# A new cycle for each pair of image rows: denominator first, double PSUM buffers, the Newton step in place

## The chip, the cores and the metric

The kernel runs on one core of a Trainium2 chip. Its engines are TensorE (PE, matmuls into the accumulator memory PSUM), VectorE (DVE), ScalarE (ACT), GpSimd (POOL), and the queue that issues transfers (SP). Each runs its own instruction stream in order, and they meet at semaphores. The metric is device time in microseconds (us); less is better.

## The reference

Two equal layers work on x of shape (2, 256, 256, 384): batch, rows h, width w, channels c, in float32. Each normalizes in 32 groups of 12 channels and adds a ratio of box sums:

```
def _gn(v, G=32, eps=1e-5):               # mean and variance over (h, w, channels of a group)
    return ((g - m) / jnp.sqrt(s + eps)).reshape(v.shape)
def conv(x):                              # windows (1, 5, 20) over h, w, c
    s = box_sum(x, 2, 5)
    num = box_sum(s * s, 3, 20)
    d = box_sum(box_sum(x * x, 2, 5), 3, 20)
    return nan_to_num(num / (d * norm))   # norm: how many columns the window of 5 covers
x = x + conv(_gn(x));  x = x + conv(_gn(x))
```

## The kernel before, in words

There are four phases: two layers times two images. A phase walks through 128 pairs of rows; four pairs make a tile, which is loaded and stored in one transfer of 3 MB. One pair is 128 partitions by 4 segments (two rows, each in two halves of the width) by 384 channels.

For one pair, POOL subtracts the group means (`centred`, L323). ACT squares it (`square`, L382). PE sums along the width: three S units on the centred rows and three T units on the squares, one per 128 channels, each into a width bank of PSUM (`width_unit`, L482). ACT copies these out, S squared and scaled into `sT` (L401), T scaled into `tT` (L398). PE sums along the channels (`channel_unit`, L506): four D units from `tT` into the denominator banks, four N units from `sT` into the numerator banks, one per segment. ACT forms a first reciprocal of the denominator by Ln and Exp (`invert`, L411 and L414). DVE makes one Newton step and the product: `approach` (L668) writes denominator times reciprocal into `newton`, `weigh` (L674) multiplies the numerator into `recip`, and `divide` (L686) writes (newton - 2) * recip, the negative ratio, for the whole pair into `y_out`. POOL subtracts it from the input (`add_ratio`, L332), and SP stores the tile.

The order of each engine is written out by hand as a list of names in its `step`: S, T, D, N as above with the number of the unit, F for parts of the next phase's statistics, L for invert, Q for squares. Channel units of a pair are mixed with the width units of the next pair. A float32 matmul of the program stands in the trace as two.

Apart from that DVE gathers group statistics with BATCH_NORM_STATS instructions, for the phase after next. In the first layer it measures each output tile (`measure_output`), eight groups per pair. In phase 0 it also measures the second image's input (`measure_beside`), eleven, eleven and ten groups in three pairs of four. At a few places `lane_totals` (BATCH_NORM_AGGREGATE) sums up what was gathered. Once per phase `ask_means` and `finish` turn this into the next phase's means and scales, with small matmuls (F1, F2, F3) and two activations (`finish_logs`). In the first 306 us only the first image is measured.

## Time and profile before

| | us |
|---|---|
| median of 3 runs | 6079.46 (6078.21 to 6080.62) |
| the profiled execution | 6080.48 |
| its span in the trace | 6078.8 |

The span runs from the first instruction to the last. A time in the trace counts from its start, and "L506" is line 506 of the kernel before. Matmuls overlap each other, so that the sum of their mean durations is above PE's busy time; weight loads (PEld) run beside them. The clock column is the part of 2.4 GHz that TensorE was granted.

### The profile page before, as it was taken

How to read it: one execution, taken by the hardware profiler on the slowest of the kernel's cores; microseconds unless marked ns; L12 is line 12 of the kernel's file. 1: busy time of each engine (PE TensorE's matmuls, PEld its weight loads, DVE VectorE, ACT ScalarE, POOL GpSimd, SP SyncE). 2: the span in 40 equal slices, each digit the busy share in tenths (PEclk: the TensorE clock that was granted, in tenths of full speed). 3: DMA queues.
4: the chain of work that ended last, by engine and by line, in shares of the span. 5: the costliest groups of instructions: out<-in, count | busy, mean ns of one | idle time of the engine just before them, and what ended most of it. 6: DMA issues, size and time to landing. Idle time of an engine off the chain costs nothing.

```text
span 6078.8 us, 138073 instructions
## 1 busy us (share of the span) xinstructions
PE 5725.4 (94%) x49196; PEld 5713.1 (94%) x49196; DVE 4097.6 (67%) x8521; ACT 5015.7 (83%) x8201; POOL 3547.4 (58%) x1043
## 2 busy tenths in 40 slices
PE   0099999999999999999999999999999999999999
PEld 0099999999999999999999999999999999999999
DVE  7888889988877676766767555555555555555555
ACT  0088888888888888888888888888888888888888
POOL 0056665566656666666665666666666666666665
PEclk9999999999999999999999999999999999999999
DMA  9956565556533434434344343343434434343343
GB/s 358 346 205 215 203 214 200 205 202 215 207 125 125 163 127 143 146 124 162 128 143 147 125 153 137 135 155 124 164 126 145 146 126 164 124 155 135 135 154 124
DMA packets 664736, 1007.80 MB, mean 166 GB/s; under 512 B 5168, under 2 KB 664624, under 8 KB 664624
## 3 DMA queue, kind: packets, MB, share of 16 engines
q1 hardware_dynamic: 664624, 1006.65, 47.2%
q14 instruction: 84, 0.69, 0.0%
q8 instruction: 28, 0.46, 0.0%
HBM read 603.98 MB, written 402.65 MB: 166 GB/s over the span
## 4 chain that ended last, share of the span: by engine, by line
PE 89%; DVE 6%; DMA 2%; issue 1%; ACT 1%; SPq 0%; POOL 0%; DVEq 0%; POOLq 0%; ACTq 0%
PE width_ps L482 43%; PE den_ps L506 23%; PE num_ps L506 23%; DVE out_stats L571 2%; DMA y_both<-in_x_dram 1%; DVE lane_mv L578 1%; DMA x_both<-in_x_dram 1%; DVE y_both L686 1%; DVE newton L668 1%; DVE recip L674 0%; DVE beside_stats L571 0%; DVE lane_mv L584 0%; SPq L204 0%; ACT recip L411 0%; ACT recip L414 0%
## 5 line engine op out<-in xcount | busy, mean ns | idle before, releaser
L323 POOL TENSOR_TENSOR centred<-x_both,mean_row 128x1536 f32<-128x1536 f32 x512 | 1771.5, 3460 | 1405.8 <-PE width_ps L482 1091.4
L332 POOL TENSOR_TENSOR y_both<-x_both,y_both 128x1536 f32<-128x1536 f32 x512 | 1771.7, 3460 | 1119.0 <-DVE y_both L686 1119.0
L668 DVE SCALAR_TENSOR_TENSOR newton<-den_ps,recip 128x384 f32<-128x384 f32 x2048 | 1112.5, 554 | 1883.5 <-ACT recip L414 1853.8
L506 PE MATMUL den_ps<-band_c,tT 128*128 128x138 f32 (+2 forms) x12288 | 1809.4, 283 | 10.7 <-DVE newton L668 10.3
L506 PE MATMUL num_ps<-band_c,sT 128*128 128x138 f32 (+2 forms) x12288 | 1732.9, 284 | 21.0 <-DVE recip L674 20.9
L482 PE MATMUL width_ps<-band_w,centred 128*128 128x130 f32 x12288 | 1629.7, 275 | 2.9 <-POOL centred L323 2.9
L482 PE MATMUL width_ps<-band_wc,square 128*128 128x130 f32 x12288 | 1625.7, 275 | 0.7 <-ACT sT L401 0.7
L506 PEld LDWEIGHTS den_ps<-band_c,tT 128*128 128x128 f32 x12288 | 1609.5, 190 | 14.5 <-DVE newton L668 12.3
L506 PEld LDWEIGHTS num_ps<-band_c,sT 128*128 128x128 f32 x12288 | 1580.8, 190 | 28.0 <-DVE recip L674 23.4
L401 ACT ACTIVATE sT<-width_ps,rstd_col 128x512 f32<-128x512 f32 x1536 | 1036.7, 675 | 591.6 <-PE width_ps L482 589.9
L482 PEld LDWEIGHTS width_ps<-band_w,centred 128*128 128x128 f32 x12288 | 1508.5, 191 | 3.0 <-POOL centred L323 3.0
L482 PEld LDWEIGHTS width_ps<-band_wc,square 128*128 128x128 f32 x12288 | 1504.1, 191 | 0.9 <-ACT sT L401 0.9
L414 ACT ACTIVATE recip<-recip,bias_exp 128x384 f32<-128x384 f32 x2048 | 1260.8, 616 | 66.3
L411 ACT ACTIVATE recip<-den_ps,bias_ln 128x384 f32<-128x384 f32 x2048 | 1184.9, 579 | 64.8 <-PE den_ps L506 18.1
L674 DVE SCALAR_TENSOR_TENSOR recip<-num_ps,recip 128x384 f32<-128x384 f32 x2048 | 1086.7, 548 | 1.1 <-PE num_ps L506 1.1
L398 ACT ACTIVATE tT<-width_ps,rvar_col 128x512 f32<-128x512 f32 x1536 | 1040.1, 677 | 1.9 <-PE width_ps L482 1.9
L686 DVE SCALAR_TENSOR_TENSOR y_both<-newton,recip 128x1536 f32<-128x1536 f32 x512 | 902.9, 1764 | 22.9
L382 ACT ACTIVATE square<-centred 128x768 f32<-128x768 f32 x1024 | 849.2, 829 | 3.4 <-POOL centred L323 3.4
L571 DVE BATCH_NORM_STATS2 out_stats<-y_both 128x192 f32 (+2 forms) x2304 | 674.2, 366 | 15.7 <-DMA y_both<-in_x_dram 15.6
L457 PE MATMUL num_ps<-stat_two,over_p 128*128 128x32 f32 x32 | 6.2, 322 | 308.0 <-DVE stat_two L621 307.1
L457 PEld LDWEIGHTS num_ps<-stat_two,over_p 128*128 128x128 f32 x32 | 5.4, 241 | 308.9 <-DVE band_wc L615 305.9
L571 DVE BATCH_NORM_STATS2 beside_stats<-beside 128x192 f32 (+1 forms) x960 | 273.7, 345 | 0.2
(45 smaller groups left out, 270.5 us busy)
## 6 DMA issues: line engine op xcount, KB each, us to landing
x_both<-in_x_dram SPq DMA_DIRECT2D x80, 3072.0 KB, 10.9
first_layer_out<-y_both SPq DMA_DIRECT2D x64, 3072.0 KB, 18.2
x_both<-first_layer_out SPq DMA_DIRECT2D x64, 3072.0 KB, 10.9
out_dram<-y_both SPq DMA_DIRECT2D x63, 3072.0 KB, 18.2
beside<-in_x_dram SPq DMA_DIRECT2D x30, 3072.0 KB, 10.9
y_both<-in_x_dram SPq DMA_DIRECT2D x18, 3072.0 KB, 18.8
out_dram<-y_both SPq DMA_DIRECT2D x4, 768.0 KB, 3.5
```

The source lines that it names most:

```text
L323: nc.gpsimd.tensor_tensor(centred[e % 2][:], x_in[slot][:, g * PSEG:(g + 1) * PSEG, :], mean_row[ph % 2][:].unsqueeze(1).to_broadcast([P, ...
L332: nc.gpsimd.tensor_tensor(y_out[slot][:, g * PSEG:(g + 1) * PSEG, :], x_in[slot][:, g * PSEG:(g + 1) * PSEG, :], y_out[slot][:, g * PSEG:( ...
L398: nc.scalar.activation(tT[par][:, k, :], src, ACT.Copy, scale=rvar_col[ph][:, k:k + 1]).then_inc(width_taken, 1)
L401: nc.scalar.activation(sT[par][:, k, :], src, ACT.Square, scale=rstd_col[ph][:, k:k + 1]).then_inc(width_taken, 1)
L411: nc.scalar.activation(recip[par][:, i, :], den_ps[i % 3][:, 0:C], ACT.Ln, bias=bias_ln[:], scale=LN_SCALE).then_inc(log_done, 1)
L414: nc.scalar.activation(recip[par][:, i, :], recip[par][:, i, :], ACT.Exp, bias=bias_exp[:], scale=-1.0).then_inc(recip_done, 1)
L482: last = nc.tensor.matmul(bank[:, at:at + WN], data[:, r * 2 + j, P * k:P * (k + 1)], band[:, j, :], start=(r == 0 and j == 0), stop=(r == ...
L506: last = nc.tensor.matmul(bank[:, lo:hi], data[:, k, at:at + P], band_c[k][:], start=(k == 0), stop=(k == KB - 1), skip_group_check=True)
L571: last = nc.vector.bn_stats(stats[:, g, bass.ds(column * 6, 6)], tile[:, :, CG * g:CG * (g + 1)])
L668: nc.vector.scalar_tensor_tensor(newton[:, i, :], den_ps[i % 3][:, 0:C], TINY, recip[par][:, i, :], ALU.add, ALU.mult).then_inc(den_used, 1)
L674: nc.vector.scalar_tensor_tensor(recip[par][:, i, :], num_ps[i % 2][:, 0:C], TINY, recip[par][:, i, :], ALU.add, ALU.mult).then_inc(num_us ...
L686: nc.vector.scalar_tensor_tensor(y_out[slot][:, g * PSEG:(g + 1) * PSEG, :], newton[:], 2.0, recip[e % 2][:], ALU.subtract, ALU.mult).then ...
```

## The change

PSUM has eight banks. Before, three held width sums, three the denominators of one segment each, and two the numerators. Now two hold width sums, two double buffers of two banks hold the denominators of two segments each, and one double buffer holds the numerators of two segments. ACT and DVE work on two segments at a time. `newton` is gone: `approach` writes its result over the denominator in PSUM, a new `correct` finishes the reciprocal in `recip`, and `weigh` multiplies it with the numerator straight into `y_out`; `divide` is gone. The squares are one activation instead of two. The T units (squares) now come before the S units, and only their copies have to be done before D0. The statistics of an output tile come in two halves per pair, and the means of a phase's end use a denominator buffer and ask later.

```
-        newton = sb("newton", [P, PSEG, C])
-        width_ps = [... [P, 2 * W] ... for i in range(3)]
-        den_ps = [... [P, 512] ... for i in range(3)]
-        num_ps = [... [P, 512] ... for i in range(2)]
+        width_ps = [... [P, 2 * W] ... for i in range(2)]
+        den_ps = [... [P, 2, 512] ... for i in range(2)]
+        num_ps = ctx.enter_context(nc.psum_tensor("num_ps", [P, 2, 512], F32))
...
@@ gpsimd, add_ratio
-                    pool.wait_ge(ratio_done, ph * NPAIR + p + 1)
+                    pool.wait_ge(num_used, (ph * NPAIR + p + 1) * 2)
...
@@ scalar
+                    nc.scalar.activation(square[par][:], centred[par][:], ACT.Square).then_inc(rows_squared, 1)
...
+                def invert(ph, p, par, h):
+                    halves = (ph * NPAIR + p) * 2 + h + 1
+                    if not is_opening(ph, p, 2):
+                        act.wait_ge(num_used, (ph * NPAIR + p - 2) * 2 + h + 1)
+                    act.wait_ge(den_done, halves)
+                    both = recip[par][:, 2 * h:2 * h + 2, :]
+                    nc.scalar.activation(both, den_ps[h][:, :, 0:C], ACT.Ln, bias=bias_ln[:],
                                          scale=LN_SCALE).then_inc(log_done, 1)
+                    act.wait_ge(log_done, halves)
+                    nc.scalar.activation(both, both, ACT.Exp, bias=bias_exp[:], scale=-1.0).then_inc(recip_done, 1)
...
-                    for what in ("S0", "L0", "T0", "L1", "S1", "Q0", "T1", "L2", "Q1", "S2", "T2", "L3"):
+                    for what in ("T0", "L0", "G0", "T1", "T2", "Q0", "S0", "L1", "S1", "S2"):
...
@@ tensor
-                    u = 2 * k + is_t
+                    u, pair = (k if is_t else KB + k), ph * NPAIR + p
+                        pe.wait_ge(width_taken, pair * UNITS + u - 1)
...
+                    pair, h = ph * NPAIR + p, i // 2
+                    if i == 0:
+                        pe.wait_ge(width_taken, pair * UNITS + (UNITS if is_num else KB))
                     if is_num:
+                        bank, data = num_ps[:, i % 2, :], sT[par]
+                        if i % 2 == 0 and not (is_opening(ph, p, 1) and h == 0):
+                            pe.wait_ge(num_used, pair * 2 + h)
                     else:
+                        bank, data = den_ps[h][:, i % 2, :], tT[par]
+                        if i % 2 == 0 and not is_opening(ph, p, 1):
+                            pe.wait_ge(den_used, pair * 2 + h - 1)
...
-                    for what in ("S0", "F1", "D0", "F2", "T0", "D1", "S1", "F3", "N0", "T1", "D2", "S2", "N1", "T2",
-                                 "D3", "N2", "N3"):
+                    for what in ("F1", "D0", "T0", "D1", "F2", "T1", "N0", "F3", "T2", "N1", "D2", "S0", "D3", "S1",
+                                 "N2", "S2", "N3"):
...
@@ vector
                 def ask_means(ph):
+                    if ph > 0:
+                        dve.wait_ge(den_used, (pairs_before(ph - 1) + finish_pair(ph - 1)) * 2)
...
+                def approach(ph, p, par, h):
+                    dve.wait_ge(recip_done, (ph * NPAIR + p) * 2 + h + 1)
+                    near = den_ps[h][:, :, 0:C]
+                    nc.vector.scalar_tensor_tensor(near, near, TINY, recip[par][:, 2 * h:2 * h + 2, :],
+                                                   ALU.add, ALU.mult).then_inc(near_done, 1)
+                def correct(ph, p, par, h):
+                    dve.wait_ge(near_done, (ph * NPAIR + p) * 2 + h + 1)
+                    both = recip[par][:, 2 * h:2 * h + 2, :]
+                    nc.vector.scalar_tensor_tensor(both, den_ps[h][:, :, 0:C], 2.0, both, ALU.subtract, ALU.mult
+                                                   ).then_inc(den_used, 1)
+                def weigh(ph, p, i, e, h):
+                    slot, at = e // PAIRS, (e % PAIRS) * PSEG + 2 * h
+                    dve.wait_ge(num_done, (ph * NPAIR + p) * 2 + h + 1)
+                    dve.wait_ge(den_used, (ph * NPAIR + p) * 2 + h + 1)
...
+                    nc.vector.scalar_tensor_tensor(y_out[slot][:, at:at + 2, :], num_ps[:, :, 0:C], TINY,
+                                                   recip[e % 2][:, 2 * h:2 * h + 2, :], ALU.add, ALU.mult
+                                                   ).then_inc(num_used, 1)
...
+                            measure_beside(ph, i, lo, e, 0)
                             approach(ph, p, par, 0)
+                            measure_beside(ph, i, lo, e, 1)
+                            correct(ph, p, par, 0)
+                            weigh(ph, p, i, e, 0)
+                            measure_beside(ph, i, lo, e, 2)
+                            measure_output(ph, i, lo, e, 0)
                             approach(ph, p, par, 1)
+                            correct(ph, p, par, 1)
                             if finishing:
                                 ask_means(ph + 1)
+                            weigh(ph, p, i, e, 1)
                             if finishing:
                                 finish(ph + 1)
+                            measure_output(ph, i, lo, e, 1)
```

On PE the units of a pair change places. These are the first rows of one pair of the opening body before (S0, D0, T0, D1, S1 are `width_ps` and `den_ps` units; a D or N unit is three rows):

```order
L482 MATMUL width_ps<-band_w,centred 128x130 x4
L506 MATMUL den_ps<-band_c,tT 128x138
L506 MATMUL den_ps<-band_c,tT 128x147
L506 MATMUL den_ps<-band_c,tT 128x137
L482 MATMUL width_ps<-band_wc,square 128x130 x4
L506 MATMUL den_ps<-band_c,tT 128x138
L506 MATMUL den_ps<-band_c,tT 128x147
L506 MATMUL den_ps<-band_c,tT 128x137
L482 MATMUL width_ps<-band_w,centred 128x130 x4
L506 MATMUL num_ps<-band_c,sT 128x138
L506 MATMUL num_ps<-band_c,sT 128x147
L506 MATMUL num_ps<-band_c,sT 128x137
```

and the first rows of the same pair after:

```order
L509 MATMUL den_ps<-band_c,tT 128x138
L509 MATMUL den_ps<-band_c,tT 128x147
L509 MATMUL den_ps<-band_c,tT 128x137
L485 MATMUL width_ps<-band_wc,square 128x130 x4
L509 MATMUL den_ps<-band_c,tT 128x138
L509 MATMUL den_ps<-band_c,tT 128x147
L509 MATMUL den_ps<-band_c,tT 128x137
L485 MATMUL width_ps<-band_wc,square 128x130 x4
L509 MATMUL num_ps<-band_c,sT 128x138
L509 MATMUL num_ps<-band_c,sT 128x147
L509 MATMUL num_ps<-band_c,sT 128x137
L485 MATMUL width_ps<-band_wc,square 128x130 x4
```

The pair now begins with D0, its T units come first, and N0 follows D1 and T1 instead of S1.

On DVE this is one whole pair of phase 0 with statistics before (approach twice, weigh, and so on to divide and the output's eight statistics):

```order
L668 SCALAR_TENSOR_TENSOR newton<-den_ps,recip 128x384 x2
L674 SCALAR_TENSOR_TENSOR recip<-num_ps,recip 128x384
L571 BN_STATS beside_stats<-beside 128x6 x3
L668 SCALAR_TENSOR_TENSOR newton<-den_ps,recip 128x384
L674 SCALAR_TENSOR_TENSOR recip<-num_ps,recip 128x384
L571 BN_STATS beside_stats<-beside 128x6 x3
L668 SCALAR_TENSOR_TENSOR newton<-den_ps,recip 128x384
L674 SCALAR_TENSOR_TENSOR recip<-num_ps,recip 128x384
L571 BN_STATS beside_stats<-beside 128x6 x4
L674 SCALAR_TENSOR_TENSOR recip<-num_ps,recip 128x384
L686 SCALAR_TENSOR_TENSOR y_both<-newton,recip 128x1536
L571 BN_STATS out_stats<-y_both 128x6 x8
```

and after:

```order
L574 BN_STATS beside_stats<-beside 128x6 x3
L671 SCALAR_TENSOR_TENSOR den_ps<-den_ps,recip 128x2x384
L574 BN_STATS beside_stats<-beside 128x6 x3
L678 SCALAR_TENSOR_TENSOR recip<-den_ps,recip 128x768
L689 SCALAR_TENSOR_TENSOR y_both<-num_ps,recip 128x768
L574 BN_STATS beside_stats<-beside 128x6 x4
L574 BN_STATS out_stats<-y_both 128x6 x4
L671 SCALAR_TENSOR_TENSOR den_ps<-den_ps,recip 128x2x384
L678 SCALAR_TENSOR_TENSOR recip<-den_ps,recip 128x768
L689 SCALAR_TENSOR_TENSOR y_both<-num_ps,recip 128x768
L574 BN_STATS out_stats<-y_both 128x6 x4
```

Nine operations have become six on twice the elements, in two runs of approach, correct and weigh, with the output's statistics behind each run.

## Rows read from the trace of the kernel before

**Rows 1.** The page, busy time of each engine, share of the span, instructions.

```profile
PE 5725.4 (94%) x49196; PEld 5713.1 (94%) x49196; DVE 4097.6 (67%) x8521; ACT 5015.7 (83%) x8201; POOL 3547.4 (58%) x1043
```

**Rows 2.** Stretches: window and length, busy us (instructions) per engine, TensorE clock, DMA.

```profile
940.00:1000.00 60.00, 50.99 (x407) 50.38 (x406) 55.90 (x138) 41.50 (x69) 29.24 (x9) 0.94 0.52 184
...
1060.00:1120.00 60.00, 52.65 (x422) 50.99 (x422) 58.34 (x143) 43.28 (x72) 29.83 (x9) 0.97 0.56 198
...
1650.00:1712.00 62.00, 52.48 (x414) 51.38 (x413) 56.85 (x143) 41.22 (x71) 28.97 (x9) 0.94 0.28 99
...
1800.00:1850.00 50.00, 48.60 (x399) 46.66 (x398) 47.66 (x108) 40.55 (x67) 29.45 (x9) 1.00 0.42 146
...
3230.00:3285.00 55.00, 53.60 (x441) 51.66 (x441) 50.61 (x107) 44.28 (x74) 32.63 (x10) 1.00 0.48 169
...
3285.00:3335.00 50.00, 49.06 (x420) 48.50 (x419) 27.28 (x52) 41.89 (x71) 28.36 (x9) 1.00 0.33 115
...
4900.00:6000.00 1100.00, 1100.00 (x9502) 1100.00 (x9501) 578.56 (x891) 968.80 (x1585) 684.11 (x199) 1.00 0.40 140
...
958.40:961.70 3.30, 3.30 (x17) 3.30 (x17) 3.27 (x9) 0.69 (x1) 0.00 (x0) 0.50 1.06 371
```

**Rows 3.** Waits of PE: waiter, releaser, us in total, times, longest.

```profile
PE num_ps L506 <- DVE recip L674: 20.9, 10, 4.2
...
PE den_ps L506 <- DVE newton L668: 10.3, 17, 1.7
```

**Rows 4.** DVE in a burst, in order of time: start, us, instruction.

```profile
966.10 5.05 DVE L578 BATCH_NORM_AGGREGATE lane_mv<-beside_stats 128x2 f32<-128x96 f32 x11
...
978.17 2.17 DVE L571 BATCH_NORM_STATS2 out_stats<-y_both 128x6 f32<-128x192 f32 x8
...
981.64 5.05 DVE L578 BATCH_NORM_AGGREGATE lane_mv<-beside_stats 128x2 f32<-128x96 f32 x11
```

**Rows 5.** A quiet pair of the second layer, in order of time.

```profile
5004.68 0.62 ACT L414 ACTIVATE recip<-recip,bias_exp 128x384 f32<-128x384 f32 x1
...
5005.30 1.06 PE L482 MATMUL width_ps<-band_w,centred 128*128 128x130 f32 x8
...
5005.32 0.56 DVE L668 SCALAR_TENSOR_TENSOR newton<-den_ps,recip 128x384 f32<-128x384 f32 x1 [2.21 <-ACT recip L414]
...
5005.80 1.01 DVE L674 SCALAR_TENSOR_TENSOR recip<-num_ps,recip 128x384 f32<-128x384 f32 x2
...
5006.19 0.88 PE L506 MATMUL den_ps<-band_c,tT 128*128 128x138 f32 x6
...
5006.91 1.06 PE L482 MATMUL width_ps<-band_wc,square 128*128 128x130 f32 x8
```

**Rows 6.** Groups by line and shape: busy us, mean ns of one, idle before.

```profile
L414 ACT ACTIVATE recip<-recip,bias_exp 128x384 f32<-128x384 f32 x2048 | 1260.8, 616 | 66.3
...
L411 ACT ACTIVATE recip<-den_ps,bias_ln 128x384 f32<-128x384 f32 x2048 | 1184.9, 579 | 64.8 <-PE den_ps L506 18.1
...
L668 DVE SCALAR_TENSOR_TENSOR newton<-den_ps,recip 128x384 f32<-128x384 f32 x2048 | 1112.5, 554 | 1883.5 <-ACT recip L414 1853.8 <-issue 2.4
...
L674 DVE SCALAR_TENSOR_TENSOR recip<-num_ps,recip 128x384 f32<-128x384 f32 x2048 | 1086.7, 548 | 1.1 <-PE num_ps L506 1.1
...
L401 ACT ACTIVATE sT<-width_ps,rstd_col 128x512 f32<-128x512 f32 x1536 | 1036.7, 675 | 591.6 <-PE width_ps L482 589.9 <-DVE rvar_col L657 1.6
...
L686 DVE SCALAR_TENSOR_TENSOR y_both<-newton,recip 128x1536 f32<-128x1536 f32 x512 | 902.9, 1764 | 22.9
...
L382 ACT ACTIVATE square<-centred 128x768 f32<-128x768 f32 x1024 | 849.2, 829 | 3.4 <-POOL centred L323 3.4
...
L571 DVE BATCH_NORM_STATS2 out_stats<-y_both 128x192 f32 x1600 | 434.2, 344 | 0.0
...
L571 DVE BATCH_NORM_STATS2 out_stats<-x_both 128x384 f32 x224 | 103.7, 543 | 33.1 <-DMA x_both<-in_x_dram 32.7 <-DVE lane_mv L584 0.4
```

**Rows 7.** PE in order of time, at the opening.

```profile
322.37 0.99 PE L506 MATMUL den_ps<-band_c,tT 128*128 128x138 f32 x6 [0.41 <-ACT tT L398]
```

More of the change, by code:

```diff
@@ L430, in _ @@
                 finish_logs(0)
-                for half in range(2):
-                    squares(0, 0, 0, half)
+                squares(0, 0, 0)
                 for k in range(KB):
-                    take(0, 0, 0, k, 0)
                     take(0, 0, 0, k, 1)
-                    if k < 2:
-                        squares(0, 1, 1, k)
+                take(0, 0, 0, 0, 0)
+                squares(0, 1, 1)
+                take(0, 0, 0, 1, 0)
+                take(0, 0, 0, 2, 0)
                 for ph in range(NP_):
@@ L456, in finish_part @@
                         for half in range(2):
-                            last = nc.tensor.matmul(num_ps[part - 1][:, 0:GROUPS], over_p[:],
+                            last = nc.tensor.matmul((mean_ps, var_ps)[part - 1], over_p[:],
                                                     stat_two[:, 2 * (part - 1), half, :],
@@ L660, in finish @@
                     dve.wait_ge(params_ready, ph + 1)
-                def approach(ph, p, par, i):
-                    dve.wait_ge(recip_done, (ph * NPAIR + p) * PSEG + i + 1)
-                    if i == 0 and not is_opening(ph, p, 1):
-                        dve.wait_ge(ratio_done, ph * NPAIR + p)
-                    nc.vector.scalar_tensor_tensor(newton[:, i, :], den_ps[i % 3][:, 0:C], TINY,
-                                                   recip[par][:, i, :], ALU.add, ALU.mult).then_inc(den_used, 1)
```

133 lines of the change are left out of this document (49 added, 84 removed).

## The prediction

> **What bounds the kernel now.** I read the page's busy times first, then stretches of the span, the waits of PE (TensorE), DVE (VectorE) in the stretches where PE loses time, one quiet pair of rows in order of time, and the durations by line.
>
> PE is busy 94% of the span [rows 1]. In the second layer it is busy without a gap: 9502 matmuls in 1100 us [rows 2], 115.8 ns each; a pair has 96 of them, so a pair takes 11.11 us. The change alters neither number nor shape of the matmuls, so it can win only time in which PE stands or runs slowly. A stretch loses its length less its matmuls times 115.8 ns: 940 to 1000 us loses 12.9, 1060 to 1120 11.1, 1650 to 1712 14.1; 1800 to 1850 and 3230 to 3285 lose 3.8 and 3.9, and there is a third like them; 3285 to 3335, one of two that finish a phase's statistics, loses 1.4 [rows 2]. That is about 52 us in all. 31 of them are waits for DVE [rows 3]; most of the rest is half rate, 1.2 instead of 2.4 GHz: after a long wait 17 matmuls run in 3.3 us where 28.5 fit, clock 0.50 [rows 2], a loss of 1.7 us at each of five places.
>
> In the lossy stretches DVE has lane totals on top of its usual work. From one series of eleven totals to the next take 981.64 - 966.10 = 15.54 us, of which the totals are 5.08 [rows 4]: an ordinary pair of phase 0 costs DVE 10.46 us, which fits in 11.11, and a burst pair 15.5, which PE waits for. There are 22 burst pairs: 3, 4 and 3 in phase 0 and three times 4 milder ones later. The ceiling of any gain is the 52 us, 0.9%, and it needs either less DVE work in those pairs or more lead before PE notices.
>
> **DVE's work.** Start to start, an operation on 384 elements takes 0.46 us (two in 1.01 where one takes 0.55 [rows 5, 6]); eight of them and the 1536-element one of 1.76 [rows 6] are 5.5 us per pair. Now there are six of 768. At the rate (1764 - 548) / 1152 = 1.06 ns per element [rows 6] one takes 548 + 405 = 0.95 us. Approach, correct and weigh follow on each other with 0.03 us between (Exp ends 5005.30, newton starts 5005.32 [rows 5]), so half a pair takes 0.98 + 0.98 + 0.86 = 2.8 and a pair 5.65. That is 0.15 more; in phase 0 some 0.1 is filled by statistics between approach and correct. A burst pair costs DVE the same within 0.1 us.
>
> The unknown is approach, which reads and writes the same two PSUM banks: no row shows DVE writing PSUM. Below, it costs at least its elements with nothing fixed, 0.81 us; above, if the bank's reads and writes take turns, 0.95 + 0.81 = 1.76. I take 0.95, since the nearest row, the numerator's operation in place on SBUF, takes 548 ns, no more than the 554 of the one that writes elsewhere [rows 6].
>
> The correct step used to read SBUF alone and now reads PSUM. Statistics on SBUF grow by (543 - 344) / 192 = 1.04 ns per element, and 1764 less 1152 x 1.04 leaves 566 ns for 384 elements from SBUF, against 548 and 554 from PSUM [rows 6]: no dearer. The Trainium skill (VectorE: DVE Perf Modes, the section on the TRN2 errata) gives a PSUM source a fixed part of 120 cycles and an SBUF source 58. By it two corrections would cost 0.13 us more per pair and the 22 burst pairs 3 us, an estimate from that page; the trace does not bear it out.
>
> **The quiet pair.** Count from the start of D0, 0.72 us for a D or N unit, 0.89 for a T or S unit (5005.30 to 5006.19), and a unit's last result 0.16 after the next unit's start (5006.19 + 0.88 against 5006.91) [rows 5]. D1 ends at 2.5. Ln of 768 elements takes between 579 + 384 x 0.60 (slope from L401 to L382) = 0.81 and twice 579 = 1.16; Exp 0.85 to 1.23 [rows 6]; I take 0.90 and 0.94, near the lower ends, because the rows of ACT (ScalarE) grow less than in proportion to size. Ln ends 3.4, Exp 4.4, approach 5.4, correct 6.4, weigh 7.35. N2, which overwrites the numerator banks, comes at 8.78: lead 1.4 us. The second half's weigh ends at 12.9 and the next N0 comes at 14.3: 1.4 again. So the single numerator buffer is tightest; both ACT upper ends together (0.55) would leave 0.85, and in phase 0 three statistics between approach and correct leave 0.6. The denominators gain: D0 waits for correct, 6.4 against 11.1, where before newton ended 5005.88 and D0 began 5006.19, a lead of 0.3 [rows 5]. The two width banks: S0 at 6.3 needs T1's copy of 5.0, the next T0 at 11.8 needs S1's of 10.5: 1.3. ACT has 6 x 0.675 + 1.8 + 1.9 + 1.5 = 9.2 of 11.1 us; what it saves (some 1.3) was hidden and stays so. POOL's two operations stay; its add now starts on the second weigh, 1.8 into the next pair, and SP's store behind it shifts with it, 44 us ahead of the next use. Of the new waits, correct's for approach is the 0.03 counted, and Ln's for the weigh of two pairs ago is over by 17 us. 512 x 0 = 0 us.
>
> **The places that lose.**
> - Opening: T0 waits for a whole square (two of 829 less an overlap, 1.5 us) where S0 ran meanwhile; but D0, which began at 322.37 after a wait of 0.41 [rows 7], now needs the three T copies alone. I take -0.5 (bounds -1.2 and +1.5). In pair 0 N2 waits 0.4 behind the early statistics. In pair 4 sixteen late ones (4.3 us) stand before approach: weigh ends 10.4, N2 waits 1.6; before, this place lost a few tenths. Together +1.
> - Phase 0 bursts. Pair 56: weigh 1.8, four statistics 2.8, ten totals 7.4, three statistics 8.1, approach 9.0, statistics, correct 10.7, weigh 11.7: N2 waits 3.0, the next two 15.5 - 11.1 = 4.4 each. That is what stood there before, give or take half a microsecond; the middle burst now stands behind the second weigh, loses 2.3, 3.2, 1.8 and 1.9, and gets 1 cheaper. Half rate follows as it did. -1.
> - Three mild bursts: DVE has 5.65 + 2.1 (eight statistics [rows 4]) + 8 x 0.46 = 11.5 against 11.1. N2 waits 0.8, then 0.5 three times, 2.3 and not 3.8: here the longer lead pays. -4.
> - Finishing: the question for the means stands behind correct, F1 is first in its pair and waits 1.1 with all of PE behind it; F3 waits 1.5 for logarithms queued behind L0 on ACT, and the second weigh stands between them on DVE. 2.6 against 1.4, twice outside the bursts: +2.4.
> - Drain: with no width units between, the last pair waits through Ln, Exp and six vector operations in a row, 1.65 + 1.84 + 5.9 = 9.4 from D0 on. Before it were Ln, Exp and nine smaller operations, partly beside them. +0.7, bounds 0 and +2.
>
> Sum: +1 - 1 - 4 + 2.4 + 0.7 = -0.9 us. The profiled execution took 6080.48, 1.0 above the median 6079.46; so 6079.6 by the profile and 6078.5 against the median. About 0.2%, 12 us, is what a measurement of this kernel can tell from no change: the forecast is no change.
>
> **Rivals.**
> 1. Slower: approach at half throughput, 0.8 us more each, 1.6 per pair. For: one bank serves both streams, and no row excludes it. Against: in-place rows on SBUF are free of it. In 90 pairs of phase 0 DVE then has 12.1 us against 11.11; three of them lose 2.8, of which the fourth, lighter pair gives back 0.6: 30 x 2.2 = 66; the burst pairs add 22 x 1.6 = 35: 6180. It decides from 0.3 us per operation, where ordinary pairs of phase 0 stop fitting; from 0.2 to 0.4 it costs 10 to 24, 6089 to 6102. Chance 0.11 for all of it.
> 2. Slower: the chain from D1 to N2 outruns its 1.4 us, and PE waits twice in every pair; 0.1 us beyond costs 512 x 0.2 = 102, 6181. It needs all five durations at their upper ends. 0.03.
> 3. Faster: a double operation costs 0.1 less than worked out. Six save 0.6 per pair, 22 burst pairs 13: 6065; if the lead also swallows the start of each phase 0 burst, 6055. For: a third fewer operations. Against: the chain exposes every fixed part. 0.09.
> 4. Clock: half rate follows long waits, 1.7 us each time. If each N2 wait above 1.6 us drew one, seven more cost 12: 6090, the edge of the forecast's range. As a mechanism of the quiet pair, short waits at the two width banks would bring one such stretch per pair, 512 x 1.7 = 870, 6950; the lead of 1.3 us there speaks against any such wait, and the clock is 1.00 over 9502 matmuls [rows 2]. The Trainium skill (TensorE: Matmul & The Clock Gate, the section on psum-queue depth-cycling) has this rule: cycling through banks leaves short idle times between groups, and the clock swings. 0.02.
>
> **Numbers.** The forecast has 0.75, with 6066 to 6091 as its own range. Faster 0.10 (rival 3 and an edge of the forecast), slower 0.15 (rivals 1, 2, 4 and no more than their sum), same 0.75. From 6062 to 6100 lie the forecast, most of rival 3 and the mild part of rival 1: some 0.85.
>
> **What would show it.** Approach at 0.9 to 1.0 us (1.7 is rival 1); second-layer stretches again with 9502 matmuls in 1100 us and clock 1.00; PE waiting for DVE at num_ps only, and in no quiet pair; losses of 2.3 in the mild bursts and 2.6 at a finish; about 10.5 us of DVE per ordinary pair of phase 0. I am wrong if a wait stands in every pair, or if pairs 56 to 58 lose under 9 us.

## The result, and the profile after

The changed kernel takes 6101.63 us (median of 7 runs, 6098.60 to 6104.98) where the one before takes 6079.02 in the same series: a ratio of 1.0037, 95% interval 1.0027 to 1.0047. It is slower by 22.6 us; the forecast was no change, with 6066 to 6091 as its own range and a wide one that ended at 6100. The profiled execution took 6099.38 us, 18.9 more than that of before.

The page's busy times, the stretches and TensorE's waits of the changed kernel, for [rows 1 to 3]:

```profile
PE 5724.5 (94%) x49196; PEld 5715.3 (94%) x49196; DVE 4105.1 (67%) x6985; ACT 4585.1 (75%) x5641; POOL 3526.8 (58%) x1043
```

```profile
3285.00:3335.00 50.00, 46.27 (x384) 45.56 (x383) 31.86 (x36) 35.70 (x45) 29.80 (x9) 0.97 0.37 127
...
4900.00:6000.00 1100.00, 1100.00 (x9502) 1100.00 (x9501) 570.60 (x594) 885.36 (x1090) 680.99 (x198) 1.00 0.40 143
...
1896.80:1900.20 3.40, 3.40 (x18) 3.40 (x18) 1.49 (x7) 1.33 (x3) 0.00 (x0) 0.54 0.88 241
```

```profile
PE den_ps L460 <- DVE stat_two L626: 314.1, 4, 305.4
PE num_ps L509 <- DVE y_both L689: 39.3, 34, 4.4
...
PE den_ps L460 <- DVE stat_two L641: 2.9, 3, 1.7
PE den_ps L465 <- DVE rstd_row L656: 2.7, 2, 1.6
```

The quiet pairs are what they were: 9502 matmuls in the same 1100 us, clock 1.00, as in [rows 2]. The stretch with a phase's finish now has 384 matmuls instead of 420. The waits at the denominator banks for the approach step ([rows 3], 10.3 us) are gone, those at the numerator banks went from 20.9 to 39.3, and those at a finish have grown. Before, they were these two:

```profile
PE num_ps L457 <- DVE stat_two L621: 307.1, 3, 305.9
...
PE num_ps L457 <- DVE stat_two L636: 0.8, 1, 0.8
```

Apart from the first 305.4 us (305.9 before), in which the first image is measured, the wait for the copy that asks for the means (F1) went from 1.2 to 8.7 us, and those for the two other parts of the finish (F2 and F3) from 0.8 to 5.6. The stretch from 1896.80, behind such waits, is one at half rate (0.54, 18 matmuls) that before did not have.

The groups of VectorE and ScalarE that the prediction priced, for [rows 6]:

```profile
L671 DVE SCALAR_TENSOR_TENSOR den_ps<-den_ps,recip 128x768 f32<-128x768 f32 x1024 | 987.5, 964 | 1754.9 <-ACT recip L414 1753.1
...
L689 DVE SCALAR_TENSOR_TENSOR y_both<-num_ps,recip 128x768 f32<-128x768 f32 x1024 | 980.8, 958 | 116.0 <-DVE recip L678 19.7
L678 DVE SCALAR_TENSOR_TENSOR recip<-den_ps,recip 128x768 f32<-128x768 f32 x1024 | 978.7, 956 | 31.8
L414 ACT ACTIVATE recip<-recip,bias_exp 128x768 f32<-128x768 f32 x1024 | 958.2, 936 | 33.9
L411 ACT ACTIVATE recip<-den_ps,bias_ln 128x768 f32<-128x768 f32 x1024 | 923.1, 901 | 36.4 <-PE den_ps L509 4.0
```

These are 964, 956 and 958 ns where 950 was forecast, and 901 and 936 where 900 and 940 were. Approach in place over the same PSUM banks costs nothing extra. So the price of the new operations is not where the time went.

Taken from the start of one pair's D0 to the next in both traces, less the 11.12 us of a pair without losses, the time stands like this:

| place (pairs) | before | after | difference | forecast |
|---|---|---|---|---|
| opening: asking the means to D0, pairs 0 to 7 | 16.8 + 0.6 | 15.8 + 2.3 | +0.7 | +1 |
| nine pairs at the head of a looped body (16 to 48, 80 to 104) | 0.0 | 5.2 | +5.2 | 0 |
| bursts at 56 to 59 and 64 to 71 | 24.5 | 25.7 | +1.2 | -1, with the third burst |
| third burst and first finish (117 to 121) | 15.6 | 19.4 | +3.8 | in the -1 |
| second and third finish (135 to 137, 263 to 265) | 6.1 | 15.8 | +9.7 | +2.4 |
| three mild bursts | 12.5 | 9.7 | -2.7 | -4 |
| drain (511) | 5.5 | 6.6 | +1.1 | +0.7 |

Two places make nearly all of it: the finishes, and a stall at nine body heads that the forecast did not have at all.

### A finish in the changed kernel

The finish at pair 136 in order of time (start, us, instruction, idle time before it and its releaser):

```profile
1888.11 3.44 POOL L325 TENSOR_TENSOR centred<-x_both,mean_row 128x1536 f32<-128x1536 f32 x1 [4.24 <-PE width_ps L485]
...
1889.45 2.14 DVE L626 COPY stat_two<-lane_mv 128x64 f32<-128x64 f32 x1
...
1891.65 0.63 PE L460 MATMUL den_ps<-stat_two,over_p 128*128 128x32 f32 x4 [2.90 <-DVE stat_two L626]
...
1892.54 3.43 POOL L334 TENSOR_TENSOR y_both<-x_both,y_both 128x1536 f32<-128x1536 f32 x1 [0.99 <-DVE y_both L689]
1892.62 3.43 DVE L639 TENSOR_TENSOR stat_two<-stat_two 128x64 f32<-128x64 f32 x1
...
1896.36 0.63 PE L460 MATMUL den_ps<-stat_two,over_p 128*128 128x32 f32 x4 [1.67 <-DVE stat_two L641]
```

A copy of 64 elements lasts 2.14 us and a square of 64 elements 3.43. Both end where GpSimd's operation ends: the copy at 1891.59 (GpSimd at 1891.55), the square at 1896.05 (GpSimd at 1895.97). The kernel before has the same operations; its groups by line:

```profile
L644 DVE TENSOR_SCALAR stat_tmp<-stat_tmp 128x32 f32<-128x32 f32 x4 | 3.2, 793 | 0.1
...
L621 DVE COPY stat_two<-lane_mv 128x64 f32<-128x64 f32 x4 | 1.6, 405 | 0.0
...
L634 DVE TENSOR_TENSOR stat_two<-stat_two 128x64 f32<-128x64 f32 x4 | 0.9, 224 | 0.1
```

There the square is 224 ns, because it ran ahead of the division, and GpSimd's addition waits for that division. The change lets the second `weigh` release the addition, and the finish stands right behind `weigh`. That an operation can be held could have been read from the kernel before: its L644 has a mean of 793 ns where the tensor-scalar operation of the same size on L649 has 182 (one of its four took 2.63 us, to the end of a subtraction on GpSimd), and its copy takes from 184 to 629. The division itself, which reads two SBUF operands, took 2.13 to 2.96 us instead of 1.76 at the three places where it began with 0.5 us or more of a subtraction to go.

### The head of a body

VectorE around the head of a looped body, in the changed kernel and then in the kernel before:

```profile
770.06 0.96 DVE L689 SCALAR_TENSOR_TENSOR y_both<-num_ps,recip 128x768 f32<-128x768 f32 x1
770.94 1.13 DVE L574 BATCH_NORM_STATS2 out_stats<-y_both 128x192 f32 x4
773.86 0.88 DVE L574 BATCH_NORM_STATS2 beside_stats<-beside 128x192 f32 x3 [1.79 <-issue]
774.65 0.95 DVE L671 SCALAR_TENSOR_TENSOR den_ps<-den_ps,recip 128x768 f32<-128x768 f32 x1
```

```profile
768.26 1.76 DVE L686 SCALAR_TENSOR_TENSOR y_both<-newton,recip 128x1536 f32<-128x1536 f32 x1
769.93 2.17 DVE L571 BATCH_NORM_STATS2 out_stats<-y_both 128x192 f32 x8
772.31 1.02 DVE L668 SCALAR_TENSOR_TENSOR newton<-den_ps,recip 128x384 f32<-128x384 f32 x2 [0.20 <-issue]
```

The trace also records the loop's compare-and-branch: at 770.65 in the changed kernel, with the next record of VectorE's stream at 773.61, and at 769.34 before, with the next at 772.12. The branch takes 2.96 and 2.78 us: it was there before. Before, the division and eight statistics (3.8 us of work) were still running under it; now one `weigh` and four statistics (2.0 us) are. Of that work 2.76 us were left at the branch before and 1.42 are left now, which covers all but 0.02 of the one branch and 1.54 of the other. VectorE's time put to "issue" at these nine heads went from 2.4 to 15.5 us:

```profile
DVE beside_stats L574 <- issue: 15.5, 9, 1.9
```

```profile
DVE newton L668 <- issue: 2.4, 9, 0.5
```

In a pair without a branch VectorE does the three statistics of the side tile in the time in which it waits for Exp. At a head this time has gone to the branch, so the approach step starts at 774.65, 1.1 us later than half a pair after the one at 768.00, more than the lead of 0.6 that the forecast gives phase 0.

### The profile page after: what moved, and what is told of

The parts are those of the page before. It is cut to its first block, busy times and chain, and to the rows that moved or that the text cites. A ratio compares the mean times of both kernels' runs of the same rounds, so it can differ in the third digit from the quotient of the medians.

```text
span 6097.4 us, 132093 instructions
## 1 busy us (share of the span) xinstructions
PE 5724.5 (94%) x49196; PEld 5715.3 (94%) x49196; DVE 4105.1 (67%) x6985; ACT 4585.1 (75%) x5641; POOL 3526.8 (58%) x1043
## 4 chain that ended last, share of the span: by engine, by line
PE 69%; DVE 3%; ACT 0%; issue 0%; POOLq 0%; POOL 0%; DVEq 0%; ACTq 0%
PE width_ps L485 33%; PE den_ps L509 18%; PE num_ps L509 18%; DVE lane_mv L581 1%; DVE recip L678 1%; DVE den_ps L671 1%; DVE y_both L689 1%; DVE out_stats L574 0%; ACT recip L414 0%; ACT recip L411 0%; DVE beside_stats L574 0%; DVE stat_two L626 0%; POOLq L192 0%; POOL y_both L334 0%; DVE stat_two L639 0%
## 5 line engine op out<-in xcount | busy, mean ns | idle before, releaser
L671 DVE SCALAR_TENSOR_TENSOR den_ps<-den_ps,recip 128x768 f32<-128x768 f32 x1024 | 987.5, 964 | 1754.9 <-ACT recip L414 1753.1
L509 PE MATMUL num_ps<-band_c,sT 128*128 128x138 f32 (+2 forms) x12288 | 1813.4, 284 | 39.3 <-DVE y_both L689 39.3
L509 PEld LDWEIGHTS num_ps<-band_c,sT 128*128 128x128 f32 x12288 | 1611.7, 190 | 45.8 <-DVE y_both L689 45.1
L689 DVE SCALAR_TENSOR_TENSOR y_both<-num_ps,recip 128x768 f32<-128x768 f32 x1024 | 980.8, 958 | 116.0 <-DVE recip L678 19.7
L678 DVE SCALAR_TENSOR_TENSOR recip<-den_ps,recip 128x768 f32<-128x768 f32 x1024 | 978.7, 956 | 31.8
L414 ACT ACTIVATE recip<-recip,bias_exp 128x768 f32<-128x768 f32 x1024 | 958.2, 936 | 33.9
L411 ACT ACTIVATE recip<-den_ps,bias_ln 128x768 f32<-128x768 f32 x1024 | 923.1, 901 | 36.4 <-PE den_ps L509 4.0
L383 ACT ACTIVATE square<-centred 128x1536 f32<-128x1536 f32 x512 | 755.1, 1475 | 1.9 <-POOL centred L325 1.9
L574 DVE BATCH_NORM_STATS2 out_stats<-y_both 128x192 f32 (+2 forms) x2304 | 696.3, 367 | 14.1 <-DMA y_both<-in_x_dram 13.9
L574 DVE BATCH_NORM_STATS2 beside_stats<-beside 128x192 f32 (+1 forms) x960 | 273.6, 345 | 16.4 <-issue 15.5
```

The costliest lines, as they stand in the source:

```text
L411: nc.scalar.activation(both, den_ps[h][:, :, 0:C], ACT.Ln, bias=bias_ln[:], scale=LN_SCALE).then_inc(log_done, 1)
L414: nc.scalar.activation(both, both, ACT.Exp, bias=bias_exp[:], scale=-1.0).then_inc(recip_done, 1)
L509: last = nc.tensor.matmul(bank[:, lo:hi], data[:, k, at:at + P], band_c[k][:], start=(k == 0), stop=(k == KB - 1), skip_group_check=True)
L574: last = nc.vector.bn_stats(stats[:, g, bass.ds(column * 6, 6)], tile[:, :, CG * g:CG * (g + 1)])
L671: nc.vector.scalar_tensor_tensor(near, near, TINY, recip[par][:, 2 * h:2 * h + 2, :], ALU.add, ALU.mult).then_inc(near_done, 1)
L678: nc.vector.scalar_tensor_tensor(both, den_ps[h][:, :, 0:C], 2.0, both, ALU.subtract, ALU.mult).then_inc(den_used, 1)
```

## The experiments

Theory of the branch: the stall at nine heads is VectorE's uncovered branch. Rival, order: the statistics that now stand ahead of approach wait for their load or delay it anyway. Theory of the port: VectorE's copies and products of SBUF operands are held by a running GpSimd operation. The Trainium skill (SBUF — State Buffer, the section Who interferes with whom) states it as a lock on a pair of ports that the two engines share, taken by a VectorE operation in a two-port mode (copies and tensor-scalar operations can be in one), or by one with two SBUF inputs against a GpSimd operation that reads SBUF, and kept for the whole instruction. Rival, place: the finish is slow by its place in the pair. Each kernel was timed in five rounds beside the kernel before; ratios are to that.

### 1. VectorE's bodies written out (e1_straight)

```diff
+                    if ph == 0:
+                        peeled = list(range(BESIDE_END))
                     looped(dve, NPAIR // BODY, tiles, peeled)
```

> The changed kernel with VectorE's fifteen bodies of the first 120 pairs written out one after the other, so that VectorE takes no loop branch there; order, waits and operations unchanged. Branch theory: the nine stalls of 0.44 to 0.77 us at the head of a body (5.2 us in all) come from VectorE's branch, 2.9 us from the compare-and-branch to the next body's first instruction, which only 0.96 + 1.13 us of work now covers; without it they vanish: 6101.6 - 5.2 = 6096.4, and no idle time of VectorE put to issue ahead of the first statistics of the side tile. Rival (order theory): the three statistics of the side tile that now stand ahead of the first approach delay it by 0.8 us, or wait for their load to land; branch or not, the stalls stay: 6101.6 within 1.

Measured: 6095.68 us, ratio 1.0026 (1.0016 to 1.0036). All nine heads take 11.12 us again (5.2 us to 0.0 in the trace). VectorE at the same head:

```profile
770.00 1.13 DVE L574 BATCH_NORM_STATS2 out_stats<-y_both 128x6 f32<-128x192 f32 x4
771.05 0.86 DVE L574 BATCH_NORM_STATS2 beside_stats<-beside 128x6 f32<-128x192 f32 x3
772.62 0.97 DVE L671 SCALAR_TENSOR_TENSOR den_ps<-den_ps,recip 128x768 f32<-128x768 f32 x1 [0.71 <-ACT recip L414]
```

The three statistics follow at once and fit in the wait for Exp. Their load does not hold them, and their place ahead of approach costs nothing where there is no branch: the order theory falls.

### 2. Approach first at a head (e2_head, e8_behind)

```diff
-                            measure_beside(ph, i, lo, e, 0)
+                            head = e == 0 and not isinstance(p, int)
+                            if not head:
+                                measure_beside(ph, i, lo, e, 0)
                             approach(ph, p, par, 0)
+                            if head:
+                                measure_beside(ph, i, lo, e, 0)
                             measure_beside(ph, i, lo, e, 1)
                             correct(ph, p, par, 0)
```

> The changed kernel, but in the first pair of a looped body approach stands ahead of the three statistics of the side tile; the branch stays. Branch theory: approach then starts as soon as the branch is over, 773.86 instead of 774.65 us at the body that was read, 0.3 later than where Exp would let it, less than the 0.6 us of lead: the stalls vanish, 6096.4. Order theory: the same 6096.4. It sets the size that either theory gives, and with the straight program tells them apart.

Measured: 6099.89, ratio 1.0034 (1.0022 to 1.0047). A miss for both theories: the nine heads keep 3.4 of 5.2 us, and two heads that lost nothing (pairs 8 and 72, with no branch ahead of them) lose 0.35 each. VectorE at the same head:

```profile
773.82 0.97 DVE L671 SCALAR_TENSOR_TENSOR den_ps<-den_ps,recip 128x768 f32<-128x768 f32 x1 [1.50 <-ACT recip L414]
774.70 1.65 DVE L574 BATCH_NORM_STATS2 beside_stats<-beside 128x192 f32 x6
776.26 0.94 DVE L678 SCALAR_TENSOR_TENSOR recip<-den_ps,recip 128x768 f32<-128x768 f32 x1
```

Approach now waits for Exp alone. But with six statistics between approach and correct instead of three, correct is 0.8 later than usual, so the delay only moved: what is left is the price of the six statistics, which the two heads without a branch pay as well. The second attempt puts all nine behind the first `weigh`, and the unedited kernel ran beside it:

```diff
...
+                            if not head:
+                                measure_beside(ph, i, lo, e, 1)
                             correct(ph, p, par, 0)
                             weigh(ph, p, i, e, 0)
+                            if head:
+                                measure_beside(ph, i, lo, e, 0)
+                                measure_beside(ph, i, lo, e, 1)
                             measure_beside(ph, i, lo, e, 2)
```

> The changed kernel, but in the first pair of a looped body all nine statistics of the side tile stand behind the first weigh; the branch stays. Branch theory: with approach at the branch's end and nothing between it and correct, weigh ends 0.3 us later than without a branch, within the lead, and the second approach is 1.2 late, within its lead of 1.4: the nine stalls vanish like in the straight program, 6101.6 - 5.2 = 6096.4. If instead the statistics' load is late (order theory), they wait behind weigh as well and the second half stalls: 6099 or more. The earlier attempt with six statistics between approach and correct took away only 0.3 of 5.2 in the profile; this one says whether those six were why.

> The changed kernel itself, unedited, beside the one above on the same chip: 6101.6, from 6098 to 6105 as before; all theories agree. It is the base for the difference of the run above.

Measured: 6098.53 (1.0031, 1.0019 to 1.0043) against 6102.07 (1.0035, 1.0022 to 1.0049) for the unedited one. The nine heads lose 0.0 in the trace where the unedited kernel again loses 5.2; approach at the same head waits for Exp alone:

```profile
773.28 0.97 DVE L671 SCALAR_TENSOR_TENSOR den_ps<-den_ps,recip 128x768 f32<-128x768 f32 x1 [1.49 <-ACT recip L414]
```

The 0.3 that the expectation names for the earlier attempt is its difference over all pairs; at the nine heads it took away 1.8. The median fell by 3.5, less than that: in its profile the pairs of the second and third finish lost 1.4 more, 17.4 against 16.0. With the two intervals overlapping, the trace settles this and not the median.

### 3. The question in GpSimd's idle time (e3_ask)

```diff
+                    if part == 1 and ph > 0:
+                        pe.wait_ge(den_used, (pairs_before(ph - 1) + finish_pair(ph - 1)) * 2)
...
-                    if ph > 0:
-                        dve.wait_ge(den_used, (pairs_before(ph - 1) + finish_pair(ph - 1)) * 2)
...
+                            if finishing:
+                                ask_means(ph + 1)
                             approach(ph, p, par, 1)
                             correct(ph, p, par, 1)
-                            if finishing:
-                                ask_means(ph + 1)
```

> The changed kernel with the copy that asks for the means moved ahead of the second approach of the finishing pair, where GpSimd has no operation under way; TensorE itself waits for the second correct step before it overwrites that bank. Port theory (a VectorE copy or a product of two SBUF operands that meets a GpSimd operation is held to that operation's end): the copy takes about 0.2 us instead of 1.76 on average, F1 waits 0.7 us instead of 2.9. What is gained depends on the square of the differences behind it: 2.2 us at each of three finishes (6095) if it gets in between GpSimd's two operations, about 1 us each (6098.6) if GpSimd's addition, whose data are then ready earlier, goes in front of it and holds it again. Rival (place theory: the chain question, F1, F2, F3 is slow by its place in the pair, not by GpSimd): F1 gains what the copy's place gives, about 0.5 us each, 6100, and the copy is as long as before, 1.8 us.

Measured: 6093.46, ratio 1.0025 (1.0015 to 1.0035). VectorE, then GpSimd, at the finish at pair 136:

```profile
1883.28 0.18 DVE L626 COPY stat_two<-lane_mv 128x64 f32<-128x64 f32 x1
...
1888.04 1.00 DVE L639 TENSOR_TENSOR stat_two<-stat_two 128x64 f32<-128x64 f32 x1
1889.07 3.36 DVE L641 TENSOR_TENSOR stat_two<-stat_two,lane_mv 128x64 f32<-128x64 f32 x1
```

```profile
1885.51 3.45 POOL L325 TENSOR_TENSOR centred<-x_both,mean_row 128x1536 f32<-128x1536 f32 x1 [4.23 <-PE width_ps L487]
1888.91 3.44 POOL L334 TENSOR_TENSOR y_both<-x_both,y_both 128x1536 f32<-128x1536 f32 x1
```

The copy is 0.18 us. The square, which came sooner, was held by the subtraction until 1888.96 and got in; but the addition had started at 1888.91, and the sum behind it was held for 3.36. That fits the port theory, though the expectation had named the square, not the sum, as the one to be held; by place there is no reason why the sum should now be the long one (it had 224 ns in the unedited kernel). TensorE now waits 0.8 us at F1 and 2.5 at F2, and the pairs of the second and third finish went from 15.8 to 13.5. The median gained 8.2 us, more than the finishes explain; in the trace 1.4 of the gain is the bursts at 56 to 71 and 0.8 the heads, which the edit does not touch.

### 4. The square from PSUM (e4_psum)

```diff
+        apart_ps = den_ps[1][:, 0, C:C + 2 * GROUPS].rearrange("p (h g) -> p h g", g=GROUPS)
...
+                    link(nc.vector.tensor_tensor(apart_ps, mean_l,
                                                  mean.unsqueeze(1).to_broadcast([P, 2, GROUPS]), ALU.subtract))
-                    link(nc.vector.tensor_tensor(stat_two[:, 1, :, :], stat_two[:, 1, :, :], stat_two[:, 1, :, :],
-                                                 ALU.mult))
-                    nc.vector.tensor_tensor(stat_two[:, 2, :, :], stat_two[:, 1, :, :], var_l, ALU.add
+                    link(nc.vector.tensor_tensor(apart_ps, apart_ps, stat_two[:, 1, :, :], ALU.mult))
+                    nc.vector.tensor_tensor(stat_two[:, 2, :, :], apart_ps, var_l, ALU.add
```

> The changed kernel at the same places, but the differences from the mean are written a second time into a free stretch of the mean's PSUM bank (one more operation of 0.2 us), and the square multiplies the PSUM copy by the SBUF one and is added to the variance from PSUM, so that neither operation reads two SBUF operands. Port theory: the square takes about 0.2 us instead of 3.43 while GpSimd's addition runs beside it; F2's wait of 1.7 and most of what TensorE loses behind it go, 2 to 2.5 us at each of three finishes, with the half-rate stretch behind two of them another 0 to 3.4: 6101.6 - 7 = 6094.6, from 6091 to 6096. The copy that asks stays at 1.8 us. Place theory: the square stays long wherever its operands lie, and one more operation costs 0.2 each: 6102.

Measured: 6101.01, ratio 1.0038 (1.0025 to 1.0052). The durations came out as the port theory has them, the time did not (6091 to 6096 was expected). VectorE, then GpSimd:

```profile
1891.93 0.23 DVE L642 TENSOR_TENSOR den_ps<-den_ps,stat_two 128x64 f32<-128x64 f32 x1
1892.20 0.22 DVE L643 TENSOR_TENSOR stat_two<-den_ps,lane_mv 128x64 f32<-128x64 f32 x1
...
1894.49 0.70 DVE L651 TENSOR_SCALAR stat_tmp<-stat_tmp 128x32 f32<-128x32 f32 x1
```

```profile
1891.71 3.44 POOL L335 TENSOR_TENSOR y_both<-x_both,y_both 128x1536 f32<-128x1536 f32 x1 [0.99 <-DVE y_both L691]
```

With one operand in PSUM the square takes 0.23 and the sum 0.22 while GpSimd's addition runs from 1891.71 to 1895.15. Beside the same addition a tensor-scalar operation from SBUF to SBUF is held to 1895.19, 0.70 instead of 0.18. F2's wait is gone, but then TensorE waits for F3 (5.6 us at three places, where the unedited changed kernel had 2.7 at two): the logarithms stand behind Ln and Exp on ScalarE, as the prediction had it. One hold was hiding the other wait. A half-rate stretch in pair 4 (2.2 us more at the opening than in the unedited kernel) took some of the rest.

### 5. The three edits at once (e5_three)

> The changed kernel with three edits at once: VectorE's bodies of the first 120 pairs written out, the asking copy ahead of the second approach, square and sum of the differences from PSUM. Branch and port theory together: 5.2 us for the branches; F1 then waits 0.7 us and F2 not at all, only F3 still waits 1.5 to 2 us for the logarithms that stand behind Ln and Exp on ScalarE, so a finish costs about 4 us over two ordinary pairs instead of 8, 11 us less in three. 6101.6 - 16 = 6085.6, from 6082 to 6088. Place theory: the finishes keep their 8 us, and only the branches go: 6095. No half-rate stretch at the second and third finish by the port theory.

Measured: 6086.89, ratio 1.0012 (1.0003 to 1.0021), inside the branch-and-port range and 8 below the place theory. The heads lose 0.0 and the second and third finish 10.5. One part of the expectation missed: the third finish still has a half-rate stretch (3.4 us at 0.50, from 3324.06), and costs 6.0 us where the second costs 4.4. The copy, the square and the sum take 0.18 to 0.23 us at all four instances. The tensor-scalar operation behind them, whose median was short before, is now held each time (shortest, median and longest in ns):

```profile
L651 DVE TENSOR_SCALAR stat_tmp<-stat_tmp x4: 1784/1957/2620, 310.0 to 3320.5; 128x32 f32<-128x32 f32 x4
```

It runs beside the two logarithm activations on ScalarE, and what TensorE still waits for is F3, 5.8 us at three places.

### 6. The finish behind the division, in the kernel before (b1_late)

```diff
                             weigh(ph, p, par, 3)
+                            divide(ph, i, p, e)
                             if finishing:
-
                                 finish(ph + 1)
-                            divide(ph, i, p, e)
```

> The kernel before, with one part of the change alone: the statistics of the next phase are finished behind the division of the finishing pair (and so beside GpSimd's addition, which that division releases) instead of ahead of it. Port theory: the square and the sum, 0.22 us each before, are held to the end of GpSimd's 3.46 us addition, on top of the division's 1.76 us that they now stand behind: 5 us at each of three finishes, 6079.2 + 15 = 6094, and the line of the square shows about 3.4 us at three of its four instances. Place theory: only the division's 1.8 us each: 6084.5, and the square stays at 0.22 us.

Measured: 6095.28, ratio 1.0028 (1.0017 to 1.0039): 16 us from this one line, 15 expected. Its groups on VectorE:

```profile
L634 DVE TENSOR_TENSOR stat_two<-stat_two 128x64 f32<-128x64 f32 x4 | 10.5, 2616 | 0.1
...
L636 DVE TENSOR_TENSOR stat_two<-stat_two,lane_mv 128x64 f32<-128x64 f32 x4 | 0.9, 226 | 0.1
```

A mean of 2616 ns over four is three of 3.41 and one of 0.23. The square alone was held; the sum behind it came after GpSimd's end. The second and third finish lose 18.4 instead of 6.1. So a place behind the division, and with it beside GpSimd's addition, is enough to make this loss, with none of the rest of the change. The division's own 1.8 us per finish is part of it, but alone was expected to give 6084.5; the second and third finish also have 6.8 us each at half rate.

### 7. The finish dealt out (e6_spread), and the lane totals too (e7_totals)

```diff
-                    finishing = ph + 1 < NP_ and isinstance(p, int) and p == finish_pair(ph)
-                    for what in ("F1", "D0", "T0", "D1", "F2", "T1", "N0", "F3", "T2", "N1", "D2", "S0", "D3", "S1",
+                    finishing = ph + 1 < NP_ and isinstance(p, int) and p - finish_pair(ph)
+                    at_part = {("F1", 0): 1, ("F2", 0): 2, ("F1", 1): 3}
+                    freed = {("D2", 0): mean_ready, ("D3", 0): log_asked, ("D3", 1): params_ready}
+                    for what in ("D0", "T0", "D1", "F1", "T1", "N0", "F2", "T2", "N1", "D2", "S0", "D3", "S1",
                                  "N2", "S2", "N3"):
...
+                            if behind in (0, 1):
+                                finish(ph + 1, "bd"[behind])
```

> As the three edits at once, and the finish is dealt out: F1 and F2 stand behind D1 and N0 of the finishing pair, F3 behind D1 of the next one, VectorE's four stages of the finish stand where their data are due, and D2 and D3 wait for the reads of that bank alone. Nothing of the finish then stands in front of TensorE but its own matmuls, 1 to 2 us at each of three places instead of 8: 6101.6 - 5.2 - 18 = 6078, from 6075 to 6082, the time of the kernel before. If a stage of the finish on VectorE is still held by GpSimd there, each 3.4 us hold shows as a wait of TensorE in front of D2 or D3: 6088. If GpSimd has nothing to do with it (place theory) the question's place no longer costs, but the square keeps its length: 6088 too, with a square of 3.4 us.

Measured: 6078.75, ratio 0.9998 (0.9989 to 1.0007). TensorE waits for no part of a finish in the later phases any more; what is left, 1.74 us per finish, is its own matmuls. So of the 8.0 us that the finish at pair 136 cost in the changed kernel, 6.3 were loss: waits of 2.9 and 1.7 at F1 and F2, and 1.7 for the half-rate stretch behind them. At the third finish F1 waited 2.9, F2 0.4 and F3 1.1, with the same stretch. Two operations at the finish at pair 136 were still held (the tensor-scalar one 1.01, the last product 2.70 us), and TensorE waited for neither.

```diff
-        beside_stats = sb("beside_stats", [P, GROUPS, SPLIT * 6])
+        beside_stats = sb("beside_stats", [P, GROUPS, SPLIT * 9])
...
-            return BESIDE_END * BODY if ph == 0 else BODY
+            return BESIDE_END * BODY + PAIRS if ph == 0 else BODY
...
+                            totals_due(ph, lo, e, True)
                             measure_beside(ph, i, lo, e, 0)
```

> As e6_spread, and the lane totals, which make the bursts, are dealt out over more pairs: the first side totals over six light pairs (with eight more columns of statistics, so that the early ones are kept longer), the middle ones over eight pairs, the last side totals over four pairs behind the last load, with the first finish moved four pairs back to make room, and the three mild series as six and two per pair. That VectorE's bursts are what is left of the loss is common to all theories; in the changed kernel they cost about 50 us over the ordinary pairs (about 12, 14 and 16 in phase 0 and three times 2.9). Dealt out, the middle one should keep about 3 and the others under 1 each: 6078 - 45 = 6033, from 6030 to 6045. If only the half-rate stretches and not the totals made the loss, about 10 us go: 6068.

Measured: 6049.83, ratio 0.9952 (0.9938 to 0.9965): faster than both kernels, 29 us below the one before, though not the 46 expected. Of TensorE's waits for the numerator banks (37.6 us in e6_spread) these are left:

```profile
PE num_ps L512 <- DVE y_both L731: 16.0, 21, 3.8
```

The first and third burst fell from 14.1 and 11.2 us in e6_spread to 2.2 and 2.6, counted at the pairs to which their totals moved (59 to 87 and 120 to 123), where less than 1 each was expected. The middle one kept 8.9, not 3: seven totals at the end of pair 67 and four more at the start of 68 meet there, and that pair alone takes 16.6 us, with a half-rate stretch in it. The mild ones kept 4.6 of 9.7.

## Why the prediction was wrong

- **The quiet pair** was right: no pair without a burst, a finish or a body's head waits for the new order, with durations within 0.02 us of those assumed, for approach in place too. Rivals 1, 2 and the quiet-pair form of 4 did not happen; rival 3 had no cheaper operation. (The 1.7 us that the prediction gives a half-rate stretch does not follow from its 17 matmuls, which make 1.3; the clock does show it, 3.41 us at 0.50.)
- **Finishing** was the failed term. The forecast had F1 waiting 1.1, F3 1.5, 2.6 in all, with the finish's operations on VectorE at the few tenths they had before. It did not ask what they meet on GpSimd at their new places: the copy that asks, behind the second correct, runs into the subtraction, and the square, behind the second `weigh`, into the addition which that `weigh` releases. They are held for up to 3.43 us each. F1 waits 2.9, F2, which the forecast had at nothing, up to 1.7, and a half-rate stretch follows: a finish loses 6.3 instead of 2.6. Experiments 3, 4 and 6 show the hold from three sides. Two finishes outside bursts make +9.7 instead of +2.4; the first lies in the third burst, and no run parts the +3.8 there between the two.
- **The body heads** were left out: the forecast split the statistics of a tile in two and put side statistics ahead of approach at no cost, without asking what had covered the loop's branch. +5.2 (experiments 1 and 2).
- **The bursts** of phase 0 came out 2 us above the forecast even without the third (+1.2 at 56 to 71 where the term was -1), partly by four half-rate stretches where three stood before, and the mild ones gained 2.7 of 4. Their sizes vary by more than that between profiles (22.5 to 25.8 at 56 to 71 among the variants of the changed kernel up to e6), so the rest of this stays open.
- **Opening and drain**: +0.7 and +1.1 for +1 and +0.7.
- Together: the terms of the table add up to 19.0 us where the forecast's made -0.9. Of the difference the finishes behind pair 135 make 7.3, the heads 5.2, and phase 0's bursts with the first finish 6.0. The two profiled executions lie 18.9 apart and the medians 22.6, because the changed kernel's was one of the shorter of seven (2.3 below its median) and that of the kernel before 1.5 above its own.
- The rivals were about the steady pair, 512 times a small price; both losses came from places that occur three and nine times.

## What to carry to other kernels

When an instruction is moved, look at what runs on the other engines at its new place, not only at what it waits for: here VectorE operations of 0.2 us lasted to the end of the GpSimd operation that ran beside them, in one case an operation that their new neighbour had just released. A line whose mean is several times its smallest instance is the sign to look for in the trace of before. And work that stands at the end of a loop's body also covers the loop's branch; before it is split or moved, subtract the branch from what is left.

## What was not expected of the hardware

- GpSimd's tensor-tensor operation of 3.44 us holds, to its end, VectorE's SBUF-to-SBUF copy (2.14 instead of 0.18), the product or sum of two SBUF operands (up to 3.43 instead of 0.22) and the SBUF tensor-scalar operation (0.70 to 2.63 instead of 0.18). It does not hold the same product with one operand in PSUM (0.23), nor copies from PSUM (0.19), nor the statistics (0.34). This agrees with the rule of the Trainium skill cited above; the Trainium skill says there that the one that comes second is blocked, and here that was always VectorE: no GpSimd operation of this kind took more than 3.49 us in any run.
- In phase 0 a loop's branch on VectorE takes 2.75 to 3.06 us from the compare-and-branch to the next record (nine times in either kernel); in the later phases, whose bodies are shorter (112 or 48 operations instead of 176 in the changed kernel), it takes 0.28 to 0.32. The DMA queue that the profile calls `instruction` tells the two apart: in each of the 18 long cases one packet of 8 KB starts in it 0.98 to 1.27 us behind the compare-and-branch, and the three that start latest (1.24 us and more) go with the three longest (3.02 to 3.06); in none of the short cases does one start in that time. So the long branch goes with a load of code, though the trace does not say for which engine, and no run varies the body's length alone. What VectorE still has in its queue runs under it: the 0.20 us of idle time before shows it nearly covered, the 1.79 after not.
- VectorE's operation that reads and writes the same two PSUM banks (964 ns for 768 elements) costs the same as one that writes SBUF (958).
